# Interaction tower on one Trainium2 core: where the farthest inner pairs of two quads are multiplied, batch by batch

## What is computed

```python
e = jnp.stack([tbl_0[ids[:, 0]], ..., tbl_15[ids[:, 15]]], axis=1)      # 2048 x 16 x 256
xk = x
for i in range(3):
    z = jnp.einsum('bfe,bge->bfge', x, xk).reshape(B_, F_ * F_, E_)
    z = jnp.swapaxes(z, 1, 2)
    z = jnp.einsum('bcl,oc->bol', z, Ws[i]) + bs[i][None, :, None]
    z = jnp.sum(jax.nn.relu(z), axis=-1)
    outs.append(z)
    xk = jnp.broadcast_to(z[:, :, None], (B_, F_, E_))
h = jnp.concatenate([z, dense_ctx], axis=1)
h = jnp.maximum(h @ W_top1 + b_top1, 0.0)
h = jnp.maximum(h @ W_top2 + b_top2, 0.0)
y = h @ W_top3
```

## Time and profile before

| | us |
|---|---|
| median of 3 runs | 578.62 |
| the profiled execution, its own time | 579.74 |
| its span | 578.0 |
| VectorE busy | 542.8 (94%) |
| ScalarE busy | 498.7 (86%) |
| TensorE busy (matmul) | 476.3 (82%) |
| GpSimd busy | 467.8 (81%) |
| mean granted TensorE clock, of full speed | 0.956 |

### The profile page before, as it was taken

The page is one execution under the profiler, slowest core; times in us unless marked ns, Lnnn a source line. Parts: engine busy times, 40 slices in busy tenths (PEclk is TensorE's granted clock), DMA queues, the critical chain, the costliest instruction groups (busy, mean ns, idle before and its releaser), DMA issues.

```text
span 578.0 us, 10773 instructions
## 1 busy us (share of the span) xinstructions
PE 476.3 (82%) x3990; PEld 190.8 (33%) x3990; DVE 542.8 (94%) x326; ACT 498.7 (86%) x1471; POOL 467.8 (81%) x354
## 2 busy tenths in 40 slices
PE   5559888687888798878989788798869888789988
PEld 5213233232333333232333323233333323233324
DVE  1697999999999999999999999999999999999994
ACT  1143698999999999999999999989999999999875
POOL 6665888889888888888888889888888888888630
PEclk9689898999989989998999999799999989999979
DMA  3352212221222122212221222212212212210000
GB/s 98 92 145 74 75 56 57 63 64 56 74 58 64 56 71 72 67 56 74 62 64 56 69 60 61 73 57 82 64 56 66 61 60 74 57 54 1 1 2 0
DMA packets 14334, 35.43 MB, mean 61 GB/s; under 512 B 5493, under 2 KB 5879, under 8 KB 14266
## 3 DMA queue, kind: packets, MB, share of 16 engines
q0 software_dynamic: 12288, 33.57, 20.3%
q1 hardware_dynamic: 1994, 1.17, 0.8%
HBM read 34.71 MB, written 0.01 MB: 60 GB/s over the span
## 4 chain that ended last, share of the span: by engine, by line
DVE 38%; ACT 28%; PE 18%; issue 10%; POOL 3%; another core or an unknown queue 1%; DMA 1%; ACTq 0%; DVEq 0%; POOLq 0%
DVE prod L436 32%; ACT outer L637 15%; PE z_ps L827 8%; DVE outer L485 6%; ACT outer L627 3%; ACT sq L582 3%; POOL x_rows L342 3%; PE t_ps L790 3%; ACT relu L593 2%; ACT xt L574 2%; PE turn_ps L898 1%; PE turn_ps L902 1%; PE turn_ps L860 1%; PE zs_ps L842 1%
## 5 line engine op out<-in xcount | busy, mean ns | idle before, releaser
L436 DVE TENSOR_TENSOR prod<-t_ps,xt 128x2048 f32<-128x2048 f32 x190 | 420.8, 2281 | 11.0 <-remote 6.7
L342 POOL DMA_INDIRECT x_rows<-in_tbl,ids_sb x256 | 248.4, 970 | 73.1 <-issue 62.0
L637 ACT ACTIVATE outer<-outer,bias_sb 128x256 f32<-128x256 f32 x476 | 236.7, 518 | 3.0 <-DVE outer L485 3.0
L827 PE MATMUL z_ps<-prod,w_sb 128*32 128x512 f32 x1520 | 191.2, 622 | 37.3 <-DVE prod L436 34.3
L356 POOL TENSOR_TENSOR intra<-xt 128x1024 f32<-128x1024 f32 (+4 forms) x90 | 205.1, 2281 | 6.0 <-PE z_ps L827 4.5
L574 ACT ACTIVATE xt<-t_ps 128x512 f32<-128x512 f32 x128 | 75.2, 604 | 45.2 <-PE t_ps L790 21.7
L637 ACT ACTIVATION_READ_ACCUMULATOR outer<-outer,bias_sb 128x1 f32 x476 | 100.2, 210 | 0.0
L485 DVE TENSOR_TENSOR outer<-y_ps,z_all 128x1408 f32<-128x1408 f32 (+2 forms) x60 | 93.4, 1598 | 4.5 <-ACT outer L627 3.5
L790 PE MATMUL t_ps<-ident,x_rows 128*128 128x128 f32 x512 | 81.2, 288 | 19.0 <-DMA x_rows<-in_tbl,ids_sb 7.1
L827 PEld LDWEIGHTS z_ps<-prod,w_sb 128*32 128x32 f32 x1520 | 45.8, 111 | 124.8 <-issue 93.3
L790 PEld LDWEIGHTS t_ps<-ident,x_rows 128*128 128x128 f32 x512 | 55.9, 143 | 81.8 <-issue 59.6
(11 more groups left out here) (69 smaller groups left out, 219.1 us busy)
## 6 DMA issues: line engine op xcount, KB each, us to landing
x_rows<-in_tbl,ids_sb POOLq DMA_INDIRECT x256
w_sb<-in_w SPq DMA_DIRECT2D x1, 512.0 KB
feat<-in_dense SPq DMA_DIRECT2D x1, 128.0 KB
w_sb<-in_w SPq DMA_DIRECT2D x1, 128.0 KB
ids_sb<-in_ids SPq DMA_DIRECT2D x1, 120.0 KB
ident<-in_identity SPq DMA_DIRECT2D x1, 64.0 KB, 2.1
w_sb<-in_w0t SPq DMA_DIRECT2D x1, 64.0 KB
sel_sb<-in_sel SPq DMA_DIRECT2D x1, 48.0 KB
```

What stands on the lines that cost most here:

```text
L342: pool.indirect_dma_start(out=x_rows[:, par, f, :], out_offset=None, in_=tables[f], in_offset=bass.IndirectOffsetOnAxis(ap=ids_sb[:, NF * ...
L436: dve.tensor_tensor(prod[:, m % PROD_RING, half, :].rearrange("p (f g s) -> p f g s", f=QF, g=QF), t_ps[:, tbank(b, q, half), :, :].unsque ...
L637: act.activation(outer_of(b)[:, o // OP, o % OP, :], outer_of(b)[:, o // OP, o % OP, :], ACT.Relu, bias=bias12_sb[:, layer - 1, o:o + 1], ...
L827: mm = pe.matmul(z_ps[j * GR:(j + 1) * GR, m % 2, 0:n], w0_sb[:, half, slot, :], src[:, half, j * n:(j + 1) * n], start=(slot == 0 and hal ...
```

## The change

In batches 2 to 14 (`VECTOR_FAR`) the pair at d = 3 of quads 2 and 3 is made by VectorE: `far_pair(b, 2)` after u1 and `far_pair(b, 3)` after u4, each one instruction of 2 x 128 elements of each partition, with the first feature of the quad read from its two banks of `t_ps` and the last one from `xt`. GpSimd leaves out its instruction of 512 elements for these two quads. `VECTOR_INNER` becomes (1,), so in batches 6 and 11 GpSimd makes all inner pairs of quad 0 again. `far_pair(b, 2)` waits for the contraction "i1" of batch b-1, since it writes into the buffer that this one reads. The contraction "i1" and `copy_tile` wait for the new semaphore `far_done`.

```diff
-VECTOR_INNER = (1, 6, 11)
+VECTOR_INNER = (1,)
+VECTOR_FAR = range(2, 15)
...
+        def pool_inner(b, pair):
+
+            return INTRA // 2 * (2 * (b - 1) + pair + 1) - sum(f in VECTOR_FAR for f in range(b + pair))
+
+        def far_pairs(b, q):
+
+            return 2 * sum(f in VECTOR_FAR for f in range(b)) + q - 1
...
-                inner_pairs(b, 1, (3,))
+                if b not in VECTOR_FAR:
+                    inner_pairs(b, 1, (3,))
...
+            def far_pair(b, q):
+
+                if b not in VECTOR_FAR:
+                    return
+                if q == 2:
+                    dve.wait_ge(contracted, part(b - 1, "i1") + 1)
+                bank = tbank(b, q, 0)
+                dve.tensor_tensor(intra[:, 1, :, q - 2, (INTRA - 1) * P:], t_ps[:, bank:bank + HALVES, 0, :],
+                                  xt[:, b % 2, :, (q + 1) * QF - 1, :], ALU.mult).then_inc(far_done, 1)
...
                 multiply(b, 1)
+                far_pair(b, 2)
                 multiply(b, 2)
...
                 multiply(b, 4)
+                far_pair(b, 3)
                 multiply(b, 5)
...
-                        act.wait_ge(intra_done, INTRA * (b - 2))
+                        act.wait_ge(intra_done, pool_inner(b - 2, 1))
+                    if b - 2 in VECTOR_FAR:
+                        act.wait_ge(far_done, far_pairs(b - 2, 3))
...
-                        pe.wait_ge(intra_done, INTRA * (b - 1) + 3 * (pair + 1))
+                        pe.wait_ge(intra_done, pool_inner(b, pair))
...
+                    if pair == 1 and b in VECTOR_FAR:
+                        pe.wait_ge(far_done, far_pairs(b, 3))
```

More of the change, by code:

```diff
@@ L127, in build @@
         intra_shared = sem("intra_shared")
+        far_done = sem("far_done")
         contracted = sem("contracted")
```

## The result

The changed kernel takes **589.31 us** (587.02 to 593.76, 6 runs) where the kernel before takes 578.94 (578.14 to 581.64, 6 runs). The ratio is 1.0196, with a 95% interval of 1.0153 to 1.0239. That is slower by 10 to 11 us, outside the range. A recorded ratio is not always the quotient of the two medians (e3: 1.0214 and 1.0181; e5: 1.0118 and 1.0140).

A forecast was written before the change was run, and what follows sets the result against it. VectorE was taken to bound the kernel; +5.1 us of work less 3.7 and 0.9 filled idle gave +0.5, so 580.2 us against the profiled 579.74, and 579.3 on the median of 578.62. Range 577.6 to 582.5.

The forecast's parts named there:

- The price of the small instruction: VectorE's 26 new instructions of 256 elements: 0.334 us a piece, 8.7 us in all, bounds 7.8 to 10.9 us.
- The net of +5.1 us of work: On VectorE: 8.7 us of new instructions less 3.6 us for the quarters of batches 6 and 11.
- I cost it at nothing: GpSimd losing 13 instructions: its full frame falls from 33.88 to 32.72 us, just under VectorE's 32.90, buying little on the path.
- The cover that I named, 0.18 us a frame: GpSimd's full frame of 32.72 us stays under VectorE's 32.90; if gone, GpSimd's 7 us of present lateness absorb the shortfall.
- 4.6 us of idle filled: VectorE, frames 2 to 14: of 5.53 us idle, new work fills 3.7 directly, and half of the remaining 1.9 as well.
- Rival 1: VectorE's idle time moves instead of filling, at layer 3's piece: whole +5.1 us (583.7), partly +1.2 to +3; chance 0.33.
- Rival 2: GpSimd's lateness caused VectorE's waits in the MLP frames; all 5.5 us idle goes, giving 577.3 us; chance 0.10 in full.
- Rival 3: `far_pair(b, 2)` waits for "i1" if TensorE slips over 2.7 us; 1 us beyond gives about +5, 584; chance 0.04.
- VectorE idle for 1 to 2 us: Sign of being right: VectorE's idle time between 89 us and frame 15 is near 1 to 2 us.
- GpSimd 1 to 2 us behind VectorE's frames: Sign of being right: GpSimd's frames follow VectorE's start by 1 to 2 us.
- GpSimd waiting for contractions again: Sign of being right: GpSimd, no longer late, waits for TensorE's contractions again; no size given.
- TensorE's 0.56 us for `intra` gone: Sign of being right: the 0.56 us that TensorE waited for GpSimd in frame 9 disappears.

The follow-up runs named there:

- e3: Kernel before with GpSimd's last inner pair moved ahead of the five gathers around it, no work added or removed: 589.40 us, ratio 1.0214.
- e5: Changed kernel with GpSimd's gathers as 5, 3, 3, 3, 2, the train of five at the frame's start: 587.33 us, ratio 1.0118.
- e14: The changed kernel again, unedited, on a chip where the kernel before takes 569.99 us: 572.67 us, ratio 1.0036.
- e10: Kernel before without GpSimd's 13 inner pair instructions, which nobody makes; VectorE as before: 587.30 us, ratio 1.0150.
- e1: Changed kernel with GpSimd's gathers as 3, 3, 3, 3, 4 in place of 3, 3, 2, 3, 5: 582.77 us, ratio 1.0069.
- e8: Changed kernel with GpSimd's gathers as 4, 3, 3, 3, 3: 585.39 us over ten runs, 582.24 without three slow ones, ratio 1.0052.
- e9: Changed kernel with the five loads that end GpSimd's frame issued by SyncE as plain loads: 583.84 us, ratio 1.0060.
- e18: The kernel before, unchanged, run again for its profile: 579.15 us, ratio 0.9965 against its own other runs.
- e15: Changed kernel with gathers 3, 3, 3, 3, 4 again, on the chip where the kernel before takes 569.99 us: 572.35 us, ratio 1.0037.
- e4: Changed kernel with VectorE again making the shared inner pairs of batches 6 and 11: 591.83 us over four runs, ratio 1.0183.
- e11: VectorE makes far pairs only in batches 4, 6, 8, 10, 12, gathers 4, 3, 3, 3, 3 there, against the kernel before: 579.54 us, ratio 1.0012.
- e12: Changed kernel with the train of five as plain loads on GpSimd's queue, on a chip where before takes 571.13 us: 572.10 us, ratio 1.0025.
- e17: Changed kernel with gathers 5, 3, 3, 3, 2 again, on the chip where the kernel before takes 569.99 us: 574.81 us, ratio 1.0079.
- e16: Changed kernel with the train of five as plain loads on GpSimd's queue, where before takes 569.99 us: 572.93 us, ratio 1.0040.
- e13: Changed kernel with gathers 5, 3, 3, 3, 2 again, on a chip where before takes 571.13 us: 573.37 us, ratio 1.0025.
- e6: Kernel before plus VectorE's 26 small instructions, written to a tensor nobody reads; GpSimd unchanged: 587.40 us, ratio 1.0144.

## Why the prediction was wrong

**The price of the small instruction: right.** It lasts 0.41 us and steps by 0.33, where I had 0.417 and 0.334 (VectorE, frame 2 of the changed kernel):

```profile
100.78 0.41 DVE L485 TENSOR_TENSOR intra<-t_ps,xt 128x256 f32<-128x256 f32 x1
101.11 4.47 DVE L447 TENSOR_TENSOR prod<-t_ps,xt 128x2048 f32<-128x2048 f32 x2
```

Undisturbed frames take 32.90 us. The net of +5.1 us of work stands, and so does the removal of the quarters.

**The step that failed: "I cost it at nothing", of GpSimd's 13 instructions.** I counted what they take and not what they stand between. GpSimd's full frame was to fall from 33.88 us to 32.72. On the chip of e14 it does, 32.67. On the chips that take 579 us before it stays 33.8 to 34.1 (the changed kernel's first execution, frames 4 to 13), since what the instruction gives back is waited away at the frame's start, and ScalarE's copies and VectorE's second unit wait with it. e3 (the order alone, +2.1%), e10 (the removal alone, +1.5%) and e1, e8, e9 (the train shortened or taken elsewhere, back to +0.5 to +0.7%) show it from both sides. The price on such chips is the ratio less that of the variants, 1.96% less 0.5 to 0.7%: 7 to 8.5 us, give or take 3 by the intervals. The profiles show 4 to 6.5 of it in frames 2 to 14 (437.2 against 433.3 in e8, 431.3 in e1 and 430.7 in e9); where the rest lies is not shown. The cover that I named, 0.18 us a frame, was counted from GpSimd's own work, which no train changes. A sign of the other cost stood in the trace of before, on ScalarE at the end of frame 8's gathers, and I had not read it:

```profile
320.19 0.60 ACT L574 ACTIVATE xt<-t_ps 128x512 f32<-128x512 f32 x1 [1.20 <-PE t_ps L790]
```

TensorE's transposes for this copy end at 318.42; the copy starts 1.8 us later, 0.88 us after the end of the last gather of a train of three (319.31).

**The second step: "4.6 us of idle filled" (3.7 and 0.9).** It was mis-sized. The kernel before has 5.5 us of idle time (4.5 in e18), and the variants without the train's cost still have 3.0 to 3.8 (e9, e1, e14), where I left 0.9. So 1 to 2.5 us were filled, and the sum is +2.6 to +4.1 us, 0.45 to 0.7%. e1, e8, e9, e14 and e15 measured 0.36 to 0.69%. I let the new work eat the waits where they had stood. In e14 three of the four large waits stand just there, 0.51 to 0.52 us ahead of the layer-3 pieces of frames 6, 9 and 14, behind both new instructions; the fourth, 1.30 us, stands ahead of u1 of frame 10. All four are in frames in which TensorE's clock dipped. The dips are not the whole of it: before, the pieces of frames 9 and 14 waited 0.57 and 0.62 us in frames with a granted clock of 1.00. What keeps those waits is not shown, and of the chip of e14 there is no profile of before to compare with. Had the train cost nothing, as on the chip of e14, the change would have been 0.36% or some 2 us slower: in the range, and on the slower side, where I had put 0.38.

**Rival 1** (the idle time moves) is the nearest to what remains, with its "+1.2 to +3" if partly true. Its mechanism, a mutual wait of VectorE and ScalarE, was not tested; in e14 the idle time is there only in frames with dips of the clock. **Rival 2** (GpSimd's lateness was the cause) is refuted: in e9 GpSimd is so early that it waits 5.9 us or more in each frame, and 3.0 us of idle time stay; e10 and e4 relieve it too and gain nothing. **Rival 3** (the wait for "i1" bites) did not happen: all 26 instructions start without a wait. That the time moved to the slower side, where I had put 0.38, was mostly luck: the larger part came by a cost that was in no rival, GpSimd's gathers delaying what other engines wait for.

**My list of signs.** VectorE idle for 1 to 2 us: no, 9.5. GpSimd 1 to 2 us behind VectorE's frames: no, 4.5 in frames 8 and 9 (295.46 - 290.96), though less than the 6 to 7 before. GpSimd waiting for contractions again: yes, but I had expected that as harmless. TensorE's 0.56 us for `intra` gone: yes, no wait of TensorE for GpSimd is left among its larger ones.

**What stays open.** Why the chips of e1 to e11 show this and those of e12 to e17 do not. On the former, releases named "remote" stand in the traces and the landing times of gathers are missing; on the latter it is the other way. Whether the signals take another way there, no run shows. Whether it is the gathering by index or GpSimd's queue as such is not settled either: e9 moved the loads to SyncE on an affected chip and helped, while e12 and e16, the plain loads on GpSimd's queue, ran only on chips where there was nothing to cure. e5, e13 and e17 (+1.2%, +0.25%, +0.8%) leave the early train unclear: 2 us above the other orders on the one chip where they ran together. And the changed kernel itself ran on only one of the two chips that take 570 to 571 us before.

## What to carry to other kernels

Taking an instruction off an engine that also issues gathers joins the gathers around it. Look at the longest run of them and at who needs another engine's result just behind it, and spread them again in the same edit. Idle time of the bounding engine is not simply room for new work: of 5.5 us here 1 to 2.5 were filled, where 4.6 had been counted. And a difference measured on one chip may be that chip's: on the chip of e14 the larger part of this one did not exist.

## What the runs showed of the hardware that was not expected

- In the changed kernel's first execution five gathers in a row (1.25 us apart) go with TensorE's results taken up only about 1.1 us after the last of them, and gathers at the start with a cut stream of TensorE: 16 matmuls in 5.7 us in place of 1.92. Such late pick-ups show on the chips of e1 to e11, three of them; what a train of five at the frame's end costs was measured on two of these, +2.1% (e3) and +1.5% (e10). GpSimd's wait at the frame's start is absent in most frames of the order of before (three, an instruction, two), 0.9 us in five frames with three gathers there (e8), 1.1 in eight with four (e1), and 1.2 to 2.1 in all twelve with five (the changed kernel; over 1 us in six of twelve in e3). On two other chips none of this shows.
- The Trainium skill, page SBUF — State Buffer, section Who interferes with whom, says that "DMA never contends with a compute engine", and that TensorE and ScalarE wait for no other engine. It speaks of the memory's ports. On the chip of e14 the trace agrees: ScalarE's copy starts 0.29 us after its transposes end, with gathers running. In the changed kernel's first execution ScalarE stands idle for 2.36 us ahead of the same copy, though the code waits there for the transposes alone. No row shows a wait at a port of the memory, so this does not test the page's rule itself; it shows that a kernel's gathers can hold up TensorE's and ScalarE's work on some chips all the same.
- The same kernel takes 578.9 to 580.8 us on three chips and 570.0 to 571.1 on two, and most of that seems to lie ahead of frame 2, where gathers run in long trains: it starts at 89.3 to 92.3 us on the three and at 81.5 to 82.9 on the two (of the latter only changed kernels were profiled).
- A VectorE instruction with both operands in SBUF took 2.4 us in place of 0.95 while a GpSimd instruction of 1.30 us ran beside it (e6, frame 6).
